# First FFN layer in groups of two pairs across both column parts of the job banks, evictions by two engines, the transposed norm split by GpSimd

## What is computed

```python
# attention: 16 heads of 16; q, k, v, output projections with biases; rotary embedding on q and k
q = _apply_rope(proj(Wq, bq), cos, sin) * scale
k = _apply_rope(proj(Wk, bk), cos, sin)
attn = softmax(einsum('bhsd,bhtd->bhst', q, k))
out = einsum('bhst,bhtd->bhsd', attn, proj(Wv, bv)) ... @ Wo.T + bo
x = _layernorm(x + out)
# FFN: 256 -> 1024 -> 256, weights quantised to -1, 0, 1
h = relu(einsum('bsd,fd->bsf', x, quantize(W1)) + b1)
x = _layernorm(x + einsum('bsf,df->bsd', h, quantize(W2)) + b2)
```

## Time and profile before

| | |
|---|---|
| runs | 3648.98 us median, 3639.77 to 3649.71 |
| profiled execution | 3645.27 us, its span 3643.5 us |
| TensorE busy | 3472.8 us, 95% |
| VectorE busy | 2913.7 us, 80% |
| ScalarE busy | 2674.6 us, 73% |
| GpSimd busy | 1931.3 us, 53% |

### The profile page before, as it was taken

How to read it: one execution, slowest core, us unless ns; L and a number is a source line. 1 busy time by engine, 2 the same in 40 slices (tenths; PEclk the granted TensorE clock), 3 DMA queues, 4 the chain that set the end, 5 groups by cost and what they waited for, 6 DMA issues and landing times.

```text
span 3643.5 us, 79641 instructions
## 1 busy us (share of the span) xinstructions
PE 3472.8 (95%) x30726; PEld 1866.1 (51%) x30726; DVE 2913.7 (80%) x5619; ACT 2674.6 (73%) x5320; POOL 1931.3 (53%) x1831
## 2 busy tenths in 40 slices
PE   4899999999999999999999999999999999999974
PEld 3443555555555555555555555555555555544444
DVE  4788888888888888888888888888888888888601
ACT  2177777887787778778877887787778877877741
POOL 2143565655565556555555556565656555623335
PEclk7599999999999999999999999999999999999977
DMA  5234444344434533453444344434443444333110
GB/s 150 41 97 94 93 107 97 98 95 109 94 92 100 113 91 90 105 113 88 91 107 110 88 95 107 100 96 96 107 97 97 95 109 94 89 82 75 35 36 24
DMA packets 292284, 336.89 MB, mean 92 GB/s; under 512 B 59712, under 2 KB 241856, under 8 KB 291648
## 3 DMA queue, kind: packets, MB, share of 16 engines
q1 hardware_dynamic: 291904, 331.79, 39.9%
HBM read 193.27 MB, written 138.41 MB: 91 GB/s over the span
## 4 chain that ended last, share of the span: by engine, by line
PE 91%; ACT 3%; issue 2%; DVE 2%; POOL 2%; DMA 0%; SPq 0%; POOLq 0%; DVEq 0%; ACTq 0%
PE sc L606 32%; PE ob L623 28%; PE job L500 23%; PE ms L595 6%; ACT prob L726 3%; DVE mxp L991 1%; POOL hid_r L1053 1%; PE ms L500 0%; POOL ka L1119 0%; PE ob L500 0%; POOL hid_r L1051 0%; DMA qa<-qk_parts 0%; DVE mxp L843 0%; POOL xt_r L1034 0%; PE sc L500 0%
## 5 line engine op out<-in xcount | busy, mean ns | idle before, releaser
L843 DVE TENSOR_REDUCE mxp<-ms 128x1 f32<-128x512 f32 x4032 | 2558.9, 683 | 480.2 <-PE ms L595 450.6
L726 ACT ACTIVATE prob<-sc 128x512 f32<-128x512 f32 x4096 | 2227.0, 597 | 724.9 <-PE sc L606 655.2
L606 PE MATMUL sc<-qa,ka 50*128 50x512 f32 x4096 | 1630.6, 455 | 44.5 <-ACT prob L726 27.0
L595 PE MATMUL ms<-ka,qa 48*128 48x512 f32 x4032 | 1623.7, 459 | 2.3 <-DVE mxp L843 2.3
L606 PEld LDWEIGHTS sc<-qa,ka 50*128 50x128 f32 x4096 | 682.6, 185 | 1240.4 <-ACT prob L726 1080.2
L623 PE MATMUL ob<-prob,v_sb 128*17 128x512 f32 x8192 | 1087.9, 603 | 0.9 <-ACT at_st L732 0.2
L595 PEld LDWEIGHTS ms<-ka,qa 48*128 48x128 f32 x4032 | 682.1, 186 | 20.4 <-DVE mxp L843 15.7
L1051 POOL CAST hid_r<-hid 128x512 fp32r<-128x512 f32 x256 | 156.4, 611 | 667.4 <-ACT hid L775 667.4
L1045 POOL TENSOR_TENSOR rstd<-ve,half_sb 128x2 f32<-128x2 f32 x128 | 89.0, 695 | 478.8 <-DVE ve L880 478.8
L1053 POOL TENSOR_TENSOR hid_r<-hid,hid_r 128x512 fp32r<-128x512 f32 x256 | 326.8, 1276 | 20.5
L500 PEld LDWEIGHTS job<-h_t,w_sb 64*128 64x128 f32 x3840 | 300.9, 187 | 30.5
(11 more groups left out here) (93 smaller groups left out, 2489.1 us busy)
## 6 DMA issues: line engine op xcount, KB each, us to landing
qk_parts<-parts SPq DMA_DIRECT2D x128, 512.0 KB, 4.2
ka<-qk_parts SPq DMA_DIRECT2D x384, 128.0 KB, 4.7
qa<-qk_parts SPq DMA_DIRECT2D x384, 128.0 KB, 7.5
attention<-at_st SPq DMA_DIRECT2D x128, 256.0 KB, 3.5
v_ones<-v_st SPq DMA_DIRECT2D x64, 272.0 KB, 3.3
v_sb<-v_ones SPq DMA_DIRECT2D x64, 272.0 KB, 9.0
xt_sb<-xt SPq DMA_DIRECT2D x64, 256.0 KB, 6.6
xn<-x SPq DMA_DIRECT2D x64, 256.0 KB, 6.1
```

What stands on the lines that cost most here:

```text
L595: nc.tensor.matmul(ms[upto(b, g, NS1, at) % MS_BANKS][:, :], operand(qa, b, g, j, ROWS)[:, qt * P:(qt + 1) * P], operand(ka, b, g, j, ROWS ...
L606: nc.tensor.matmul(sc[upto(b, g, HG * STEPS, n) % SC_BANKS][:, :], operand(ka, b, g, j, ROWS + MROWS)[:, tt * P:(tt + 1) * P], operand(qa, ...
L726: nc.scalar.activation(prob[st_ % 2][:, j, :], sc[upto(b, g, HG * STEPS, n) % SC_BANKS][:, :], ACT.Exp).then_inc(s["exp_done"], 1)
L843: nc.vector.reduce_max(mxp[:, kh, j * TT + qt:j * TT + qt + 1], ms[upto(b, g, NS1, at) % MS_BANKS][:, :], AX.X).then_inc(s["s1_taken"], 1)
```

## The change

Five things are done together.

- **First FFN layer.** f0 and f1 become the two phases of one group, f2 and f3 those of the next. A group is two pairs of tiles: the first pair in the first 256 columns of both job banks, the second in the other 256. A phase has 16 matmuls, all behind score 1. The group is ready once, at the end of f1 or f3.
- **Evictions.** ScalarE empties job[0] and VectorE job[1], for e1, o1, v1, f1 and f3. ScalarE does so behind the second exponential, VectorE behind the second maximum of the step. After a group each takes two hidden tiles.
- **The transposed norm.** ScalarE writes t4 as one fp32 tile h1_f; GpSimd splits it into the high and the low part (`split_first_norm`), between rotate_even and rotate_odd. f0 waits for that.
- **Norms.** EPS is added by GpSimd in one small operation for each norm instead of two by VectorE; some statistics move by one to three parts of a step. `sum_h1` moves ahead of rotate_even.
- **Maxima.** mxp has two copies, and the combination moves from the end of step 7 to step 8, with turn, high and low one part later each.

Its core, with repetitions left out:

```diff
-IN_TWO_PLACES = ("t3", "f0", "f1", "f2", "f3")
-FIRST_NORM = {(0, 3): "sums", (1, 1): "stats 0", (1, 3): "stats 1", (2, 1): "moments 0"}
-SECOND_NORM = {(0, 0): "stats 0", (0, 2): "stats 1", (1, 1): "moments 0"}
-MAXIMA_AT = {(8, 0): "turn", (8, 1): "high", (8, 2): "low"}
+FIRST_NORM = {(0, 3): "sums", (1, 2): "stats 0", (2, 0): "stats 1", (2, 2): "moments 0"}
+SECOND_NORM = {(0, 0): "stats 0", (0, 2): "stats 1", (1, 0): "moments 0"}
+MAXIMA_AT = {(8, 0): "combine", (8, 1): "turn", (8, 2): "high", (8, 3): "low"}
...
+            def first_layer(b, g, group, phase, bank_free):
+
+                if phase == 0:
+                    pe.wait_ge(s["split_low"], upto(b, g, 1, 1))
+                    for what, n in bank_free:
+                        wait_used(pe, s[what], n)
+                for p in range(2):
+                    n = 2 * group + p
+                    terms = [[(w1_sb[:, c, f * P:(f + 1) * P], h1_t[part][:, c * TQ:(c + 1) * TQ]) for f in (2 * n, 2 * n + 1)]
+                             for c in range(KC) for part in range(2)]
+                    last = in_halves([bank[:, p * TQ:(p + 1) * TQ] for bank in job], terms, phase, p == 0, p == 1)
+                if phase == 0:
+                    return []
+                last.then_inc(s["f_ready"], 2)
+                return [(f"f_{side}_taken", upto(b, g, FT // 2, 2 * group + 2)) for side in ("even", "odd")]
...
-                if name in IN_TWO_PLACES:
+                if name[0] == "f":
+                    return first_layer(*at, int(name[1]) // 2, int(name[1]) % 2, free) if place == 1 else free
+                if name == "t3":
                     return tail_job(*at, name, place // 2, free) if place in (1, 3) else free
...
+            def take_hidden(b, g, n, tile):
+
+                act.wait_ge(s["f_ready"], upto(b, g, FT // 2, n + 1))
+                wait_used(act, s["hid_low"], upto(b, g, FT // 2, n - 1))
+                nc.scalar.activation(hid[n % 2][:, 0, :], tile, ACT.Relu, bias=b1_sb[:, 2 * n:2 * n + 1]
+                                     ).then_inc(s["f_even_taken"], 1)
...
                         exps(b, g, st_, 0)
                         exps(b, g, st_, 1)
-                        if job_ and job_[2] == "t4":
+                        if job_:
                             finish(job_)
                         exps(b, g, st_, 2)
                         exps(b, g, st_, 3)
-                        if job_ and job_[2] != "t4":
-                            finish(job_)
...
+                for tl in range(TL):
+                    nc.vector.bn_aggr(moments[:, tl, :], stats[:, tl, :]).then_inc(s["moments" + tag], 1)
...
+                    nc.vector.tensor_scalar((ev_sb, od_sb)[eo][:, 1, :], job[1][:, 0:TQ], bqk_sb[:, 1, eo:eo + 1], None, ALU.add
+                                            ).then_inc(s[full + "_taken"], 1)
...
+                nc.vector.tensor_scalar(hid[n % 2][:, 1, :], tile, b1_sb[:, 2 * n + 1:2 * n + 2], 0.0, ALU.add, ALU.max
+                                        ).then_inc(s["f_odd_taken"], 1)
...
+                                if part == 1 and stage == "proj":
+                                    take_key_half(*at, name)
+                                elif part == 1 and name in ("f1", "f3"):
+                                    for p in range(2):
+                                        take_hidden(*at, int(name[1]) - 1 + p, job[1][:, p * TQ:(p + 1) * TQ])
...
+                nc.gpsimd.tensor_tensor(var[:, :], moments[:, :, 1], eps_sb[:, :], ALU.add).then_inc(s["var" + tag], 1)
...
+            def split_first_norm(b, g):
+
+                pool.wait_ge(s["t4_taken"], upto(b, g, 2, 2))
+                wait_used(pool, s["f_ready"], upto(b, g, FT // 2, 0))
+                nc.gpsimd.tensor_copy(h1_t[0][:, :], h1_f[:, :]).then_inc(s["split_high"], 1)
+                pool.wait_ge(s["split_high"], upto(b, g, 1, 1))
+                nc.gpsimd.tensor_tensor(h1_t[1][:, :], h1_f[:, :], h1_t[0][:, :], ALU.subtract).then_inc(s["split_low"], 1)
...
                     finish_first_norm(b - 1, g)
+                    sum_h1(b - 1, g)
                 for at in proj[:1]:
                     rotate_even(pool, nc.gpsimd, *at)
+                if tail:
+                    split_first_norm(b - 1, g)
+                for at in proj[:1]:
                     rotate_odd(pool, nc.gpsimd, *at)
```

More of the change, by code:

```diff
@@ L215, in build @@
         at_st = [sb(f"at_st{i}", [P, NQ]) for i in range(QH)]
-        mxp = sb("mxp", [P, 2, HG * TT])
+        mxp = [sb(f"mxp{i}", [P, 2, HG * TT]) for i in range(2)]
         mx = sb("mx", [P, HG * TT])
@@ L745, in proj_job @@
                     wait_used(act, s["v_stored"], upto(b, g, 16, 0))
-                    for tl in range(TL):
+                    for tl in tiles:
                         done = nc.scalar.activation(
@@ L764, in tail_job @@
                     act.wait_ge(s["t4_ready"], upto(b, g, 1, 1))
+                    wait_used(act, s["split_low"], upto(b, g, 1, 0))
                     for half in range(2):
-                        nc.scalar.activation(half_of(h1_t[0], half), banks[half][:, 0:TQ].rearrange("p (k i) -> p k i", i=UPPER),
-                                             ACT.Copy).then_inc(s["t4_high"], 1)
-                if name[0] == "f":
-                    n = int(name[1])
-                    act.wait_ge(s["f_ready"], upto(b, g, FT // 2, n + 1))
-                    wait_used(act, s["hid_low"], upto(b, g, FT // 2, n - 1))
-                    for i in range(2):
-                        f = 2 * n + i
-                        done = nc.scalar.activation(hid[n % 2][:, i, :], banks[i][:, 0:TQ], ACT.Relu,
-                                                    bias=b1_sb[:, f:f + 1])
-                    done.then_inc(s["f_taken"], 1)
+                        nc.scalar.activation(half_of(h1_f, half), banks[half][:, 0:TQ].rearrange("p (k i) -> p k i", i=UPPER),
+                                             ACT.Copy).then_inc(s["t4_taken"], 1)
+                elif name[0] == "f" and end:
+                    take_hidden(b, g, int(name[1]), banks[0][:, 0:TQ])
+                elif name in ("f1", "f3"):
+                    for p in range(2):
+                        take_hidden(b, g, int(name[1]) - 1 + p, job[0][:, p * TQ:(p + 1) * TQ])
             def batch(b, tail=True, first=False):
@@ L848, in combine @@
                 wait_used(dve, s["mx_turned"], upto(b, g, 1, 0))
-                nc.vector.tensor_tensor(mx[:, :], mxp[:, 0, :], mxp[:, 1, :], ALU.max).then_inc(s["max_done"], 1)
+                nc.vector.tensor_tensor(mx[:, :], mxp[(b * G + g) % 2][:, 0, :], mxp[(b * G + g) % 2][:, 1, :], ALU.max).then_inc(s["max_done"], 1)
             def take_maxima(b, g, part):
-                if part == "turn":
+                if part == "combine":
+                    combine(b, g)
+                elif part == "turn":
                     dve.wait_ge(s["max_done"], upto(b, g, 1, 1))
@@ L935, in batch @@
                             maximum(*maximum_tiles(b, g, 4 * st_ + part, last))
-                            if part == 3 and nxt and st_ == STEPS - MAX_AHEAD - 1:
-                                combine(b + (g + 1) // G, (g + 1) % G)
                             if tail if g else tail_before:
```

115 lines of the change are left out of this document (59 added, 56 removed).

## The result

The changed kernel took 3565.51 us in the median of four runs (3562.38 to 3569.30), the kernel before 3649.31 (3639.77 to 3649.71): a ratio of 0.9777, with an interval of 0.9757 to 0.9797. The profiled execution has a span of 3567.5 us, 76.0 less than that of before.

The account below looks back on a forecast made before the run. TensorE sets the pace, its f steps waiting for exponentials. Terms: -118 + 31 + 3 + 0 + 0 + 2 - 2 = -84 us, from 3645.3 to 3561, or 3565 against the median; range from a little below 3534 to 3612.

Parts of the forecast that it names:

- (a): Four f steps of each quarter, 16 matmuls in one place after s1: 1.96 us per quarter, 118 us off.
- The rival of the restart: In f steps, the 0.47 is mostly restart of the array: 24 us off, 31 back, about 3650; chance 0.05.
- (b): ScalarE's eviction behind e1, two tiles in a row: 0.26 us each behind f1 and f3, 31 us given back.
- (c): VectorE takes the other bank: net +1.3 us of its work per quarter, cost 0.05 per quarter, 3 us.
- (d): GpSimd splits the transposed norm ahead of rotate_odd: slack 2.8 us at the first hidden tile, 0.8 at g1, no cost.
- (e): Evicting e1, o1 and v1 in mid-step, the second copy of mxp and the later combine: no cost.
- VectorE becomes what is waited for: Tiles queue behind maxima, TensorE waits 0.5 us a quarter beyond (c): 3595; chance 0.20.
- (f): First batch +2 us (0 to 4), stretch after the loop -2 us (-6 to +6).
- The rival with GpSimd a little late: GpSimd's small operations cost more and g1 waits 0.5 to 0.8 us: 3600 to 3610; chance 0.08.

Follow-up runs that it names:

- e1: Not a run: a job whose tile ScalarE and VectorE evict in mid-step, one tile each; the prediction also calls the second score's exponential e1.
- both edits: Changed kernel with the combine as a one-input reduction and ScalarE's second hidden tile behind e3: 3526.40 us, ratio to before 0.968.
- 12 + 4: Kernel with both edits, f0 and f2 cut into 12 matmuls behind score 1 and 4 behind score 3: 3551.32 us, single execution.
- e3: Not a run: ScalarE's fourth exponential of a step, made from score s3.
- a5: Kernel with both edits, output projection t3 whole behind score 1 instead of in two places: 3568.17 us, ratio to before 0.9788.
- c2: Kernel with both edits, f0 and f2 cut into 8 matmuls behind score 1 and 8 behind score 3: 3577.55 us, single execution.

## Why the prediction was right, and where it wasn't

The median came out at the forecast to a microsecond. By the parts it is less good than that; errors of both signs met.

**(a) The cut: right.** 14.32 us for the four f steps fell to 12.43 where nothing else disturbs them (both edits), against 12.36 forecast; f1 keeps the 0.1 that it had over its neighbours before. What an f step paid was waiting for exponentials, and the kernels cut 8 + 8 and 12 + 4 show it. The rival of the restart falls: it priced a cut at 0.1 a step, and cuts put back into two steps cost 0.94 a quarter. The estimate that the prediction worked out from the Trainium skill, TensorE: Matmul & The Clock Gate, section Single matmul latency, would make 39 us of the cut; 1.9 us a quarter were measured, some 110 us. So the latency of a lone matmul isn't what a cut costs here.

**(b) The give-back: right in mechanism, a little too large.** 0.26 each was forecast. g0 is 0.23 over a g step. f2 is 0.14 over it in the quarters with a short combine. Together 0.37 a quarter, 22 us for 31. Moving one tile behind e3 brings it all back (0.39).

**(c) VectorE's tiles: the size wrong, the cost right.** A hidden tile takes 0.47 us on VectorE (a pair 0.86) where I took 0.38 from the subtraction at t4. VectorE is busy 46.8 us a quarter (912 us of the 1000 in the middle of the run), 46.4 forecast. With both edits TensorE waits for it no more than before. Step 2 even gained the 0.05 that it had over its neighbours.

**(d) GpSimd: right.** It waits 3.85 us for the first hidden tile (2.8 forecast), and no g job waits for a split. The small additions were taken at 0.4 and are half of that. From the groups of instructions on the page of the changed kernel:

```profile
L1075 POOL TENSOR_TENSOR ve<-mv,eps_sb 128x2 f32<-128x2 f32 x128 | 25.0, 196 | 484.4 <-DVE mv L896 484.4
```

**(e) "The later combine: nothing, the same small instruction elsewhere" — this step failed.** It costs 0.62 us in 38 of 54 quarters, 23.6 us. The numbers to see it were in the prediction. Part (d) says that rotate_odd, which ended at 1542.89, now ends at about 1546.5, and the combine stood at 1544.01 between it and the first hidden tile at 1547.60, a stretch in which GpSimd was idle. That combine, in the trace of the kernel before:

```profile
1544.01 0.19 DVE L849 TENSOR_TENSOR mx<-mxp 128x32 f32<-128x32 f32 x1
```

I asked what the later rotate_odd does to those who wait for it, and not which instructions of another engine now run beside it. The line of all its executions in the kernel before had a sign too: a most of 1639 ns over a median of 193. Two of the 64 were long, 1.64 and 1.62 us, both in batch 0, and both began 0.8 us into a GpSimd operation of 2.4 us. The rival "VectorE becomes what is waited for" named the place of the wait (maxima) and its size (0.5 a quarter), with another cause: not the amount of VectorE's work but one held instruction.

**(f) First batch and end: partly luck.** The two spans differ by 76.0: 60.0 in the 54 steady quarters (38 at 0.93 and 16 at 1.55), 4.6 in the six behind them, 6.6 in the end stretch (2 were forecast), 9.0 in batch 0, where I had forecast a loss of 2, and 4.2 lost ahead of the first score. Of those 9.0, 8.2 are in the very first quarter. Its beginning in windows, before and after:

```profile
134.40:156.00 21.60, 20.49 (x92) 11.37 (x93) 14.81 (x24) 7.36 (x14) 2.51 (x2) 0.50 0.55 91
156.00:177.60 21.60, 20.44 (x96) 9.75 (x92) 14.91 (x24) 8.30 (x17) 8.48 (x7) 0.50 0.03 10
```

```profile
138.60:160.20 21.60, 20.47 (x92) 11.43 (x93) 15.27 (x25) 7.14 (x13) 2.50 (x2) 0.50 0.56 92
160.20:181.80 21.60, 19.10 (x118) 8.58 (x114) 19.28 (x33) 9.84 (x19) 11.09 (x8) 0.91 0.08 27
```

The granted clock is 0.50 (1.2 GHz) in the first window of both. In the second it is still 0.50 before and 0.91 on average after: there it rose to 2.4 GHz early in the window (and was at 0.50 once more from 185 to 190). The change doesn't do that. Of the traces of the experiments, nine have first quarters of 81.1 to 83.0 us, like the 83.2 of before, and seven of these nine contain the change but for their one edit, or two; a5 and c2, with the same work there, have 71.4 and 73.8, like the 75.0 of the changed kernel. A single execution can gain or lose 8 to 12 us there. The other three executions of the changed kernel were 1 to 7 us shorter than the traced one; they have no trace, so how far they owe it to the clock or to the combine isn't shown.

So quarters 4 to 63 gave 64.6 us for the 84 forecast. Missing are 24 for the combine; the smaller give-back and step 2 made up some of it, and the end and the early clock filled the sum.

**Slips in the working.** The quarters of 52.6 before and 51.2 after are 0.23 too long, as the windows of the earlier trace rows overlap the next quarter: 52.37 less the 1.4 forecast is 51.0, so the measured mean of 51.26, which seems to meet the 51.2, is 0.3 above the forecast; the long combine costs 0.44 in the mean. The rival with GpSimd a little late comes to 3595 to 3613 by its own terms, not 3600 to 3610, and the one of the restart to about 3655, not 3650. The forecast doesn't hang on any of them.

## What to carry to other kernels

When an edit moves work on one engine, list also the instructions of the other engines that will now run beside it, not only those that wait for it: here a small VectorE operation with two SBUF inputs was cheap (0.18 us) where it met no GpSimd operation that had already begun, and took up to 1.64 where it did; written with one strided input it took 0.21 at the same place in either case. Where a piece of work covers a wait, its place and its length count, and a split piece covers less; but joining the parts pays only if no change of phase remains inside and its banks are emptied in time. And read the least, median and most of an instruction that you take as free: a most of eight times the median named a collision here that a shift then made the rule.

## What was not expected of the hardware

- An operation of VectorE on 32 elements a partition took 1.33 us instead of 0.18 (two SBUF inputs, beside a GpSimd operation of 1.29 us on 512), and 0.21 as a reduction of one input of 64. It was held whether it started with GpSimd's (1516.79 both) or 0.08 behind it (1279.15 and 1279.23), for all of what was left; when it was 0.02 ahead it took 0.18, and GpSimd's took 1.32 instead of 1.29. The same kind of operation with one input in SBUF and one in PSUM was never held.
- Two 64-row halves that exchange their banks inside a run of 16 matmuls lose 0.44 us (1.39 for the 0.95 of a g job); 0.26 of it is the second phase's first load waiting for the first phase's matmuls.
- The granted clock rises from 1.2 to 2.4 GHz during the first quarter, earlier in one traced execution than in another with the same work ahead of it (in the traces 22 us behind the first score in the changed kernel, some 61 in the kernel before and in the one with both edits): the first quarter took 71 to 83 us, and the span moves with it.
